# Gates in the sorted rows, tiles weighted on their way out of PSUM, and gathers that add into the sequence

## What is computed

```python
x = x + 0.5 * ffn(layernorm(x), Wg, bg, W1, b1, W2, b2)
x = x + attention(layernorm(x))
x = x + 0.5 * ffn(layernorm(x), Wg, bg, W1, b1, W2, b2)

def ffn(x, Wg, bg, W1, b1, W2, b2):
    probs = softmax(x @ Wg + bg)                 # 8 experts
    w, idx = top_k(probs, 2)
    w = w / sum(w)
    comb = sum(one_hot(idx, 8) * w)              # two gates for each token
    h = relu(einsum('nd,edh->enh', x, W1) + b1)  # 128 -> 256
    y = einsum('enh,ehd->end', h, W2) + b2
    return einsum('end,ne->nd', y, comb)
```

## Time and profile before

| | us |
|---|---|
| median of three runs | 1019.02 |
| lowest and highest run | 1017.11, 1022.14 |
| the profiled execution's own span | 1039.1 |
| busy in it: TensorE, ScalarE, VectorE, GpSimd | 975.9, 833.7, 789.0, 529.3 |
| in the tail (113 us): TensorE, VectorE, GpSimd, ScalarE | 93.5, 96.7, 70.6, 59.0 |

### The profile page before, as it was taken

One profiled execution on the slowest core, in us unless ns is written; L12 is line 12 of the kernel. 1 busy time (PEld: TensorE's weight loads), 2 busy tenths in 40 slices (PEclk: granted clock), 3 DMA queues, 4 the chain that ended last, 5 costly groups with the idle time before them and its releaser, 6 DMA issues.

```text
span 1039.1 us, 20329 instructions
## 1 busy us (share of the span) xinstructions
PE 975.9 (94%) x6512; PEld 546.9 (53%) x6512; DVE 789.0 (76%) x2255; ACT 833.7 (80%) x1194; POOL 529.3 (51%) x623
## 2 busy tenths in 40 slices
PE   7899999999999999989999999998999998888995
PEld 5687777633332488843333323332688862246673
DVE  5799999867767789857777777776878754368997
ACT  4655553599999988879999999998999988865653
POOL 5546777744444314354677766666100006555775
PEclk8999999999999999999999999999999999899998
DMA  6444223000051234420111111261444421133443
GB/s 182 165 152 133 100 102 103 14 21 20 19 147 60 75 130 163 145 89 24 36 37 35 36 37 34 57 179 36 122 139 146 143 83 49 44 127 107 131 155 121
DMA packets 59821, 96.15 MB, mean 93 GB/s; under 512 B 9179, under 2 KB 30403, under 8 KB 59715
## 3 DMA queue, kind: packets, MB, share of 16 engines
q1 hardware_dynamic: 47568, 71.50, 21.5%
q0 software_dynamic: 10752, 22.04, 7.1%
q10 hardware_dynamic: 1396, 1.31, 0.4%
HBM read 56.36 MB, written 38.45 MB: 91 GB/s over the span
## 4 chain that ended last, share of the span: by engine, by line
PE 53%; ACT 18%; issue 11%; DVE 10%; POOL 3%; DMA 3%; another core or an unknown queue 1%; SPq 0%; ACTq 0%; POOLq 0%; DVEq 0%
ACT probs L2023 10%; PE ps L1764 10%; PE ps L1749 6%; ACT sums L2023 5%; DVE low L1007 3%; PE ps L1375 3%; PE ps L1377 3%; PE ps L1376 2%; PE ps L1361 2%; PE ps L1386 2%; PE ps L1387 2%; PE ps L1391 2%; PE ps L1398 2%; PE ps L732 2%; PE ps L734 2%
## 5 line engine op out<-in xcount | busy, mean ns | idle before, releaser
L2023 ACT ACTIVATE probs<-ps 128x1024 f32<-128x1024 f32 x344 | 337.1, 1126 | 20.4 <-PE ps L1749 20.0
L1704 POOL DMA_INDIRECT found<-tiles,home x168 | 168.2, 1001 | 198.7 <-ACT sums L2023 126.9
L1692 POOL DMA_INDIRECT sorted<-xn,slot x168 | 168.1, 1000 | 179.2 <-ACT probs L2023 63.0
L1764 PE MATMUL ps<-probs,value 128*32 128x512 f32 x1376 | 185.2, 610 | 3.1 <-ACT probs L2023 1.4
L2023 ACT ACTIVATE sums<-ps 128x1024 f32<-128x1024 f32 x168 | 173.8, 1127 | 7.8 <-PE ps L1749 6.9
L1749 PE MATMUL ps<-shared 32*128 32x512 f16 x1024 | 144.7, 387 | 20.5 <-ACT probs L2023 6.8
L1188 ACT ACTIVATE high<-ps 128x512 fp32r<-128x512 f32 x176 | 101.1, 593 | 74.3 <-PE ps L734 58.7
L1007 DVE SCALAR_TENSOR_TENSOR low<-ps,high 128x512 fp32r<-128x512 f32 x176 | 113.0, 682 | 11.2 <-ACT high L1188 10.2
L1749 PEld LDWEIGHTS ps<-shared 32*128 32x128 f16 x1024 | 37.9, 91 | 157.8 <-ACT probs L2023 72.1
L1264 POOL TENSOR_TENSOR sums<-sums 128x512 f32<-128x512 f32 x59 | 76.6, 1298 | 66.6 <-DVE sums L1039 48.5
L1764 PE MATMUL ps<-sums,value 128*32 128x512 f32 x672 | 90.9, 613 | 0.2 <-ACT sums L2023 0.2
(11 more groups left out here) (202 smaller groups left out, 1869.2 us busy)
## 6 DMA issues: line engine op xcount, KB each, us to landing
found<-sorted SPq DMA_DIRECT2D x56, 256.0 KB
tiles<-sums SPq DMA_DIRECT2D x56, 256.0 KB
probs<-gates SPq DMA_DIRECT2D x24, 512.0 KB
wide<-gates SPq DMA_DIRECT2D x20, 512.0 KB
sorted<-zeros SPq DMA_DIRECT2D x16, 512.0 KB
out<-X SPq DMA_DIRECT2D x15, 256.0 KB
sorted<-xn,slot POOLq DMA_INDIRECT x168
found<-tiles,home POOLq DMA_INDIRECT x168
```

The lines of the kernel that those rows point to most:

```text
L1692: nc.gpsimd.indirect_dma_start(sorted_rows[group_of(q)], bass.IndirectOffsetOnAxis(ap=slot[:, q % XNS, k, j:j + 1], axis=0), xn[:, rows_sl ...
L1704: nc.gpsimd.indirect_dma_start(found[:, q % 2, k, j, :], None, tile_rows[group_of(q)], bass.IndirectOffsetOnAxis(ap=home[:, q, k, j:j + 1] ...
L1764: ins = nc.tensor.matmul(ps[q * W:(q + 1) * W, MIX, :], value[:, s % 2, sd, j, m, q, :], ring[ring_at(g * UNITS + 2 * j + q // 2)][:, q % ...
L2023: nc.scalar.activation(ring[ring_at(n)], ps[:, score_banks(n), :], ACT.Exp, scale=SCORE).then_inc(sm["a_probs"], 1)
```

## The change

A sorted row gets a 129th column that holds its gate (`ROW`). `route_gates` writes the first gate straight into `xn`; before the fifth send of a sequence GpSimd waits until the first four have landed, copies the second gate over the first one, and sends the other four. When a tile has been loaded, GpSimd copies its 512 gates into `tile_gates` (`keep_gates`, one instruction of 128x4 a tile), and `copy_out` multiplies by them as it leaves PSUM. `collect` then gathers with an add, straight into `X`; `found`, `combine_half`, `scale_half`, `add_half` and their tables are gone. Two gathers into the same tokens may not overlap, so GpSimd waits before the fifth gather of a sequence until the first four have landed, and in the second layer `collect_at` puts four gathers of another sequence between the two halves. `route_gates` moves from quarter 1 to quarter 0.

```diff
+ROW = D + 1
+GATHERS = 3
+GATED = 8
...
-COMBINED = {(14, 2): 0, (15, 0): 1, (15, 2): 2, (15, 3): 3}
 COLLECTS = [(2, 2, 2, 2, 2, 2, 2, 2)] * 3 + [(2, 2, 2, 2, 2, 2, 0, 0)]
-ADDED = {(0, 3): 8, (0, 4): 9, (0, 7): 10, (1, 0): 11, (1, 3): 12, (1, 4): 13, (1, 7): 14, (2, 0): 15,
-         (2, 3): 16, (2, 4): 17, (2, 7): 18, (3, 0): 19, (3, 3): 20, (3, 4): 21}
 
 ADDS = 1, 3, 4, 5
 LAST_ADDS = 1, 3, 4, 5, 6, 7
 
 def tile_slot(t):
 
-    return (tile_at(t) + 2 * (GROUP[1] % 2)) % 4
+    return tile_at(t) % 4
+
+
+def collect_at(c):
+
+    block, j = divmod(c, J)
+    if block == 0 or (block % 2 == 1 and block < 2 * NJOBS[1] - 1):
+        return GROUP[1] + (block + 1) // 2, j
+    return GROUP[1] + (block - 1) // 2, J + j
...
-        xn = sb("xn", [P, XNS, J, D])
+        xn = sb("xn", [P, XNS, J, ROW])
...
-        found = sb("found", [P, 2, TOPK, J, D])
-        scratch = found[:, 1, :, :, :].rearrange("p k j d -> p (k j d)")
...
+        def all_added(eng, q):
+
+            eng.wait_ge(gathered[q % GATHERS], 16 * TOPK * J * (q // GATHERS + 1))
...
-                    reached(sp, sm["c_added"], GROUP[y] - 1)
-                if tile_at(t) == 2:
-                    reached(sp, sm["c_added"], GROUP[y])
                 reached(sp, sm["t_turned"], t - 3)
+                reached(sp, sm["t_gates"], t - 3)
                 at = nc.sync.value_load(row[0:1, y, tile_at(t):tile_at(t) + 1], min_val=0, max_val=ROWS - T)
-                sp.dma_start(tile_rows_in[:, tile_slot(t), :],
+                sp.dma_start(tile_rows_in[:, tile_slot(t), :, :].rearrange("p j d -> p (j d)"),
                              sorted_rows[y][bass.ds(at, T), :].rearrange("(p j) d -> p (j d)", j=J)).then_inc(tile_in[tile_slot(t)], 16)
...
             def store_sorted(q):
-                sp.wait_ge(sm["c_added"], q + 1)
+                all_added(sp, q)
...
-                if e == (7 if n == WHOLE - 1 else 4):
+                if e == (7 if n == WHOLE - 1 else 3):
                     route_gates(dve, early_at(n - 2))
...
-                    if (n - WHOLE, e) in ADDED:
-                        at = ADDED[n - WHOLE, e]
-                        add_half(dve, GROUP[1] + at // TOPK, at % TOPK)
...
-                        scale_half(act, GROUP[1] + at // TOPK, at % TOPK)
...
-                            collect(pool, GROUP[1] + at // (TOPK * J), at % (TOPK * J))
+                            collect(pool, *collect_at(at))
...
-            nc.vector.tensor_scalar(gates[:, q, 0, :], rinv[:, :], 0.5, None, ALU.mult).then_inc(sm["r_gate_one"], 1)
-            nc.vector.scalar_tensor_tensor(gates[:, q, 1, :], second[:, u, :], 0.5, rinv[:, :], ALU.mult, ALU.mult).then_inc(sm["r_gates"], 1)
+            nc.vector.tensor_scalar(xn[:, rows_slot(q), :, D:ROW], rinv[:, :].unsqueeze(2), 0.5, None, ALU.mult).then_inc(sm["r_gate_one"], 1)
+            nc.vector.scalar_tensor_tensor(gates[:, q, :], second[:, u, :], 0.5, rinv[:, :], ALU.mult, ALU.mult).then_inc(sm["r_gates"], 1)
...
-        def combine_half(dve, q, k):
...
-        def scale_half(act, q, k):
...
-        def add_half(dve, q, k):
...
-                nc.vector.tensor_copy(tile_out[:, t % 2, :], ps[:, TILE_BACK, :]).then_inc(sm["t_out"], 1)
+                dve.wait_ge(sm["t_gates"], t + 1)
+                nc.vector.tensor_tensor(tile_out[:, t % 2, :].rearrange("p (j d) -> p j d", j=J), ps[:, TILE_BACK, :].rearrange("p (j d) -> p j d", j=J),
+                                        tile_gates[:, t % GATED, :].unsqueeze(2).to_broadcast([P, J, D]), ALU.mult).then_inc(sm["t_out"], 1)
...
                 pool.wait_ge(sm["r_slot"], q + 1)
+                pool.wait_ge(sm["r_gate_one"], q + 1)
                 if q + 1 in GROUP:
                     pool.wait_ge(tail_cleared[group_of(q)], 16 * E)
+            if n == J:
+
+                pool.wait_ge(sent[q % XNS], 16 * (TOPK * J * (q // XNS) + J))
+                pool.wait_ge(sm["r_gates"], q + 1)
+                nc.gpsimd.tensor_copy(xn[:, rows_slot(q), :, D:ROW], gates[:, q, :].unsqueeze(2)).then_inc(sm["r_second_gate"], 1)
+                pool.wait_ge(sm["r_second_gate"], q + 1)
             k, j = n // J, n % J
             nc.gpsimd.indirect_dma_start(sorted_rows[group_of(q)], bass.IndirectOffsetOnAxis(ap=slot[:, q % XNS, k, j:j + 1], axis=0),
                                          xn[:, rows_slot(q), j, :], None).then_inc(sent[q % XNS], 16)
                 pool.wait_ge(sm["g_home"], group_of(q) + 1)
                 if q in GROUP:
                     tiles_stored(pool, TILE0[group_of(q) + 1])
-                    pool.wait_ge(sm["t_turned"], TILE0[group_of(q) + 1])
-                reached(pool, sm["c_added"], q - 1)
+                reached(pool, gathered[q % GATHERS], 16 * TOPK * J * (q // GATHERS))
+            if n == J:
+
+                pool.wait_ge(gathered[q % GATHERS], 16 * (TOPK * J * (q // GATHERS) + J))
             k, j = n // J, n % J
-            nc.gpsimd.indirect_dma_start(found[:, q % 2, k, j, :], None, tile_rows[group_of(q)],
-                                         bass.IndirectOffsetOnAxis(ap=home[:, q, k, j:j + 1], axis=0)).then_inc(gathered[q % 2], 16)
-
+            nc.gpsimd.indirect_dma_start(tokens(sorted_seq(q), j, 1), None, tile_rows[group_of(q)],
+                                         bass.IndirectOffsetOnAxis(ap=home[:, q, k, j:j + 1], axis=0), compute_op=ALU.add).then_inc(gathered[q % GATHERS], 16)
+
+        def keep_gates(pool, t):
+
+            pool.wait_ge(tile_in[tile_slot(t)], 16 * loads_of_slot(t))
+            reached(pool, sm["t_out"], t - GATED + 1)
+            nc.gpsimd.tensor_copy(tile_gates[:, t % GATED, :].unsqueeze(2), tile_rows_in[:, tile_slot(t), :, D:ROW]).then_inc(sm["t_gates"], 1)
...
+                if hg == 0 and earlier is not None:
+                    route_gates(dve, earlier)
                 if hg == 0 and more:
                     if WHOLE <= s + 1:
-                        dve.wait_ge(sm["c_added"], s + 2 - WHOLE)
+                        all_added(dve, s + 1 - WHOLE)
...
-                if hg == 3 and WHOLE <= s + 2 < S:
-                    combine_half(dve, s + 2 - WHOLE, 0)
-                    combine_half(dve, s + 2 - WHOLE, 1)
-                if (s, hg) in COMBINED:
-                    combine_half(dve, GROUP[1] + COMBINED[s, hg], 0)
-                    combine_half(dve, GROUP[1] + COMBINED[s, hg], 1)
...
-            for q in range(GROUP[1], GROUP[1] + EXTRA):
-                for n in range(TOPK * J):
-                    pool.wait_ge(sm["t_low"], min(C * (STEPPED * (q - GROUP[1]) + 7) + n, C * TILE0[1]))
-                    send(pool, q, n)
+            for i in stream(0, TILE0[1]):
+                if in_stream(i + 2, 0, TILE0[1]):
+                    keep_gates(pool, i + 2)
+                for q in range(GROUP[1], GROUP[1] + EXTRA):
+                    for n in range(TOPK * J):
+                        lows = min(C * (STEPPED * (q - GROUP[1]) + 7) + n, C * TILE0[1])
+                        if (lows + 1) // C - 2 == i:
+                            pool.wait_ge(sm["t_low"], lows)
+                            send(pool, q, n)
...
-            scale_half(act, SORTED - 1, 0)
-            scale_half(act, SORTED - 1, 1)
...
-            add_half(dve, SORTED - 1, 0)
             last_add(dve, 0)
             last_add(dve, 1)
-            add_half(dve, SORTED - 1, 1)
```

More of the change, by code:

```diff
@@ L253, in build @@
         ones16 = sb("ones16", [P, P], F16)
-        zeros = sb("zeros", [P, D])
+        zeros = sb("zeros", [P, ROW])
         ident = K[:, IDENT:IDENT + P]
@@ L304, in build @@
         rinv = sb("rinv", [P, J])
-        gates = sb("gates_sorted", [P, SORTED, TOPK, J])
+        gates = sb("gates_sorted", [P, SORTED, J])
         zrowf = sb("zrowf", [P, E])
@@ L1989, in attn_vector @@
                     route_copy_rows(dve, job)
-                if hg == 1 and earlier is not None:
-                    route_gates(dve, earlier)
                 if hg == 0 and job is not None and late(s):
@@ L2127, in _ @@
                 attn_gpsimd(pool, half // 2, half % 2)
[L2128 to L2131 removed]
+            for i in stream(0, TILE0[1]):
[7 more added lines that the diff above has]
+                            send(pool, q, n)
             for half in range(2 * TILED, PAUSES[1] // 2):
                 attn_gpsimd(pool, half // 2, half % 2)
[L2134 to L2135 removed]
+            for i in stream(TILE0[1], TILE0[2]):
+                if in_stream(i + 2, TILE0[1], TILE0[2]):
+                    keep_gates(pool, i + 2)
+                if i == TILE0[1] + 1:
+                    norm_pool(pool, "f_", WHOLE, place(WHOLE))
+                if i == TILE0[1] + 2:
+                    norm_pool(pool, "f_", WHOLE + 1, place(WHOLE + 1))
             for half in range(PAUSES[1] // 2, 2 * S):
@@ L2231, in first_stream @@
                     route_slots(dve, extra_at(i, 5))
-                if extra_at(i, 6) is not None:
-                    route_gates(dve, extra_at(i, 6))
```

(4 more changed lines are left out.)

54 lines of the change are left out of this document (13 added, 41 removed).

## The result

| | us |
|---|---|
| before, median of four runs | 1019.5 (1017.1 to 1022.1) |
| after, median of four runs | 1101.3 (1096.9 to 1102.7) |
| ratio after / before, 95% interval | 1.079 (1.076 to 1.082) |
| span of the profiled execution after | 1100.4 |

I had forecast 1013.8, with 1030 as the upper end. The profile shown ahead of the prediction caught an execution some 20 us longer than usual (its second attention stage, the transition and its tail are longer). A second profile of the same kernel has a span of 1017.9 us, 2 us under its time as in all variants, and stages are compared with that one from here on.

The account below looks back on a forecast made before the run. ScalarE was taken to pace attention, TensorE's stops and nearly full GpSimd the tail. 5.7 us gained in tail and transition, less 0.5 ahead of tile stream 2, is 5.2: 1019.0 - 5.2 = 1013.8 us, range 1009 to 1030.

Parts of the forecast that it names:

- What bounds the kernel: Attention paced by ScalarE's exponentials, savings there 0; in the tail TensorE's stops, and GpSimd with about 4 us free in 75.
- The gain: Tail with transition: TensorE's path 5.7 us shorter, GpSimd's 6.2 less 46c; the shorter gain, 5.7, counts.
- The three stops of 4.74 us: Tail: three TensorE stops behind VectorE's additions and a scaling, 4.74 us together, expected to go.
- the rival of waits that only move: Tail: TensorE's stops covered by others, only the end's 3.3 us remain, less 0.5: 1016.2 us; chance 0.10.
- The price c: GpSimd's extra time for each gather with an add: taken as 0, upper bound 0.50 us.
- The rival of the third address: Each gathered row's third address costs GpSimd up to 0.50 us a gather: 1036.3 us, slower; chance 0.24.
- The landing: GpSimd's wait for four gathers before the fifth: 5.2 us of other gathers against a 2.57 us landing, hidden, 0.
- The end: End of the tail: the last store follows the last gather's landing directly, 3.3 us sooner on GpSimd's path.
- The rows of 516 bytes: Rows of 516 bytes instead of 512 move 0.8% more, counted as 0.
- The sends and gates: Wait and gate copy before the fifth send, hidden except ahead of tile stream 2: 0.5 us lost, between 0.2 and 1.
- The tiles: Tile streams: gate copies on idle GpSimd, and weighting in place of a PSUM copy of the same size, cost 0.

Follow-up runs that it names:

- e8: Changed kernel without its gates: rows of 512 bytes, no gate copies or weighting, plain gathers that overwrite, so only the sums are removed; 1016.2 us, ratio 0.996.
- e12: Kernel before, with gathers that add in the second layer only (96 of the 168); 1061.8 us, ratio 1.040.
- e1: Changed kernel with plain gathers that overwrite instead of adding, every wait and place kept; 1044.3 us, ratio 1.025.
- e2: Changed kernel with the table of sorted rows cleared in pieces of 4128 bytes instead of 516; 1078.8 us, ratio 1.059.
- e6: Changed kernel with rows that start 640 bytes apart in DRAM instead of 516; 1078.4 us, ratio 1.058.
- e5: Changed kernel with plain gathers that overwrite and the clearing in large pieces (e1 and e2 together); 1024.4 us, ratio 1.006.
- e13: e5 with sends in attention spread so that GpSimd has three, not four, ahead of the next sequence's squares; 1019.4 us, ratio 1.000.

## Why the prediction was wrong, step by step

- **What bounds the kernel**: right for the tail's GpSimd path (4 us free in 75), wrong in its conclusion for attention. I read that ScalarE paces it and VectorE waits, and counted everything there at 0; I never looked at what GpSimd's order does to VectorE and to the next sequence's norm. Attention 5 to 13 lost 33 us, 13 of them by the clearing.
- **The gain**: the tail's 5.7 us was 5.5 in the stages, though of the time only 3.4 arrived (e8). The agreement is partly luck. TensorE's path got 8.1 us shorter and not 5.7, and GpSimd's, which ruled, 5.4: the waits for VectorE fell by 3.8 us where I had 2.9, the gathers by 1.7, and the end gave nothing of its 3.3. The three stops of 4.74 us that I read belong to the longer execution, too; in the second profile TensorE waits 4.5 us for L1039 in nine pieces, the longest 0.9. That e8's 1016.2 is the number of the rival of waits that only move is luck as well, for that rival kept nothing but the 3.3 us of the end.
- **The price c**: this is the step that failed worst. I took 0 because a gather and a scatter cost the same; they both copy, so that row said nothing of a third access. It is 0.59 us, above even my upper bound of 0.50. The rival of the third address was right in direction, and its own formula with 0.59 gives 1019.0 + 0.5 - 6.2 + 46 x 0.59 = 1040.4; that it is an address for each row is not shown, the runs show the time and 144 packets instead of 32. It was short as well because it counted the 46 gathers behind 954 us alone, where 62 to 69 stand in the tail: e12 shows that the second layer's adds cost 41 to 43 us, the first layer's 19.
- **The landing**: right for the tail. A gather with an add is issued at 1092.19 in the changed kernel, and the store follows at 1095.39: 3.20 us, of which 1.55 are the instruction, so 1.65 remain, against 2.57 - 0.98 = 1.59 before. e1 keeps every landing wait, and the loss is not in them; those beside the clearing cost much, and elsewhere in the changed kernel the longest idle time put down to a gather's landing is 1.2 us.

```profile
1092.19 1.55 POOL L1683 DMA_INDIRECT X<-tiles,home  x1 [0.30 <-issue]
1095.39 0.33 SPq L501 DMA_DIRECT2D out<-X  x1
```

- **The end**: wrong. The store follows the last landing, as forecast, but the store doesn't end the program; GpSimd's DRAIN does. From the start of the last plain gather to the end of the span it is 10.4 us before and 10.3 in e8, so the term was worth 0 and not 3.3.
- **The rows of 516 bytes**: I counted 0.8% more bytes and wrote 0. They cost 22.5 us, by where the rows start and by one transfer that I had not listed among the changed ones: the clearing, whose landing holds a send (e2, e6).
- **The sends and gates**: 0.5 us forecast, 8.2 measured (e5 - e8), of which e13 gives 5.0 back (1024.4 - 1019.4) by order alone. I checked that each wait was short, and not where it pushes what is queued behind it on GpSimd: in e5 the copies of `value` fall beside VectorE's work on `wide`, 0.6 us a sequence.
- **The tiles**: right. The weighting takes 688 ns, the copy before 686, and tile stream 2 is 0.5 us longer in e5 than in e8.

## What to carry to other kernels

A transfer that does arithmetic is priced by running one, not by the transfers that copy: where the engine that issues the gathers has no time left, moving sums into them makes it the limit. On an engine with time to spare, an added wait or instruction still shifts what stands behind it, so ask what will then run beside which instruction of another engine, and compare the lengths of both. A term for the end of the program needs the row of the engine that finishes last, which need not be the one that stores. When an experiment comes out as expected, look in its trace whether the step that it was to move is the one that moved. Widening a row by one word changes where every row starts, so list every transfer of that table, the clearing too, and keep the rows' pitch a round number.

## What the runs showed of the hardware

- A gather of 128 rows of 512 bytes that adds into SBUF takes GpSimd 1588 ns against 1001, and 144 packets against 32; the landing after the instruction takes the same 1.6 us at the end of the tail.
- Pieces of 516 bytes written to DRAM at a pitch of 516 moved at about 130 GB/s, at a pitch of 640 at about 265; pieces of 512 at a pitch of 512 at about 280.
- GpSimd's closing DRAIN ended 9.1 us after the end of its last plain gather in eight profiles, and 6.4 us after that of the last adding one in six.
- GpSimd's copies of 128x256 beside VectorE's work on `wide` took 1.61 us a pair and VectorE's three instructions 2.8; apart they took 0.78 and 2.1.
